# Sorting a step's matmuls by tile shape: quarter taps, masks and scores ahead of the whole taps of the first convolution

## What is computed

```python
stk = _neighborhood(x)                      # 9 shifted views, zero padded
q = einsum('bhwd,de->bhwe', x, Q_P)
k = einsum('bhwkd,de->bhwke', stk, K_P)
v = einsum('bhwkd,de->bhwke', stk, V_P)
scores = einsum('bhwke,bhwe->bhwk', k, q) * mask
alpha = softmax(scores, axis=-1)
t = x + einsum('bhwk,bhwke->bhwe', alpha, v)
t_in = t
t = relu(conv(t, ff1_kernel) + ff1_bias)
t = relu(conv(t, ff2_kernel) + ff2_bias)
t = relu(conv(t, ff3_kernel) + ff3_bias)
return t_in + t
```

## Time and profile before

| | |
|---|---|
| Median of 3 runs | 2202.69 us (2202.68 to 2203.93) |
| The profiled execution | 2203.28 us |
| Its span, first to last instruction | 2201.5 us |
| TensorE busy (PE) | 2143.1 us, 97% of the span |
| VectorE busy | 1875.5 us, 85% |
| ScalarE busy | 1121.7 us, 51% |
| A middle step, first r_product to the next | 32.93 us |
| Granted TensorE clock, mean | 0.997 |

### The profile page before, as it was taken

The page is one execution under the profiler, slowest core; times in us unless marked ns, Lnnn a source line. Parts: engine busy times, 40 slices in busy tenths (PEclk is TensorE's granted clock), DMA queues, the critical chain, the costliest instruction groups (busy, mean ns, idle before and its releaser), DMA issues.

```text
span 2201.5 us, 62613 instructions
## 1 busy us (share of the span) xinstructions
PE 2143.1 (97%) x24057; PEld 1206.6 (55%) x24057; DVE 1875.5 (85%) x2772; ACT 1121.7 (51%) x3059; POOL 17.8 (1%) x28
## 2 busy tenths in 40 slices
PE   3999999999999999999999999999999999999998
PEld 2655555555555555555556555555556555555554
DVE  4888888888888888888878888888888888888886
ACT  2554554554544555555545555545545554554552
POOL 3000000000000000000000000000000000000000
PEclk9999999999999999999999999999999999999999
DMA  5445445445444445455444454454455454454453
GB/s 135 120 145 162 145 138 162 145 137 163 146 138 152 140 153 153 140 151 155 141 145 146 130 174 143 130 173 143 131 172 148 134 165 147 132 165 149 138 158 127
DMA packets 288996, 323.26 MB, mean 147 GB/s; under 512 B 88996, under 2 KB 222948, under 8 KB 282340
## 3 DMA queue, kind: packets, MB, share of 16 engines
q1 hardware_dynamic: 288940, 322.45, 49.0%
HBM read 152.50 MB, written 33.82 MB: 85 GB/s over the span
## 4 chain that ended last, share of the span: by engine, by line
PE 92%; DVE 5%; issue 1%; DMA 1%; SPq 1%; ACT 0%; DVEq 0%; ACTq 0%
PE conv_banks L505 32%; PE conv_banks L530 27%; PE conv_banks L460 16%; PE mix_bank L438 6%; PE score_banks L411 4%; DVE work L893 3%; PE score_banks L423 3%; PE mix_bank L450 3%; PE score_banks L403 1%; DMA work<-w 1%; PE mix_bank L387 0%; ACT relued L720 0%; DVE dt L821 0%; SPq L270 0%; ACT prob L663 0%
## 5 line engine op out<-in xcount | busy, mean ns | idle before, releaser
L505 PE MATMUL conv_banks<-dodd,w3f 128*64 128x512 f32 (+2 forms) x1616 | 499.9, 591 | 4.8 <-DVE work L860 3.1
L505 PE MATMUL conv_banks<-deven,w3f 128*64 128x512 f32 (+2 forms) x1616 | 492.1, 580 | 0.0
L663 ACT ACTIVATE prob<-score_banks,negmax 128x100 f32<-128x100 f32 x1040 | 344.2, 343 | 196.2 <-DVE negmax L783 196.2
L460 PE MATMUL conv_banks<-dt,w1f 128*64 128x256 f32 (+2 forms) x4128 | 384.8, 387 | 8.1 <-DVE work L893 1.4
L530 PE MATMUL conv_banks<-duh,w2h 64*128 64x512 f32 (+1 forms) x1576 | 323.2, 403 | 0.8 <-DVE work L884 0.6
L530 PE MATMUL conv_banks<-duh,w2l 64*128 64x512 f32 (+1 forms) x1576 | 314.5, 392 | 0.0
L460 PEld LDWEIGHTS conv_banks<-dt,w1f 128*64 128x64 f32 (+1 forms) x4128 | 205.1, 135 | 185.8 <-issue 57.9
L530 PE MATMUL conv_banks<-dul,w2h 64*128 64x512 f32 (+1 forms) x1576 | 280.5, 402 | 0.0
L505 PEld LDWEIGHTS conv_banks<-dodd,w3f 128*64 128x64 f32 x1616 | 137.4, 136 | 231.1 <-issue 211.6
L680 ACT COPY probt<-score_banks 100x1024 f32<-100x1024 f32 x130 | 132.0, 1015 | 242.2 <-PE score_banks L423 242.2
L675 ACT COPY rq<-mix_bank 128x512 f32<-128x512 f32 x65 | 38.2, 588 | 406.9 <-PE mix_bank L387 406.8
(11 more groups left out here) (96 smaller groups left out, 2919.1 us busy)
## 6 DMA issues: line engine op xcount, KB each, us to landing
xk<-x_keys SPq DMA_DIRECT2D x66, 800.0 KB
xc<-x_bands SPq DMA_DIRECT2D x66, 650.0 KB, 4.9
xr<-x_bands SPq DMA_DIRECT2D x264, 128.0 KB, 3.4
dodd<-dodd SPq DMA_DIRECT2D x65, 512.0 KB, 5.1
out<-work SPq DMA_DIRECT2D x64, 512.0 KB, 2.7
xs<-x_bands SPq DMA_DIRECT2D x132, 128.0 KB, 3.1
dt<-dt SPq DMA_DIRECT2D x65, 256.0 KB, 2.3
deven<-deven SPq DMA_DIRECT2D x65, 256.0 KB, 5.5
```

The source lines that it names most:

```text
L460: mm = nc.tensor.matmul(bank[(LOWER, UPPER)[o], n * 256 + lo * 64:n * 256 + hi * 64], w1f[i][rows, m, s, o * C:o * C + C], dt[rows, lo + s ...
L505: mm = nc.tensor.matmul(bank[rows, lo_ * 128:hi_ * 128], w3f[:, m, s, odd * C:odd * C + C], source[:, lo_ + s // 2:hi_ + s // 2, m], start ...
L663: last = nc.scalar.activation(prob[:, g % 2, a], score_banks[:, g % 2, a * KEYS:(a + 1) * KEYS], ACT.Exp, bias=negmax[:, g % 2, a:a + 1], ...
```

## The change

- **TensorE, a step with k from 1 to 15.** After r_product and the first masks come the inner quarter taps, the scores of half 0, the second masks, the scores of half 1 and the outer quarter taps, all 64*64. Then all whole taps, inner and outer, and directly behind them the four tiles of the third convolution, all 128*64. The turn of half 0 stands behind the third convolution. Both halves of mix stand together behind the first half of the second convolution. v_product stands behind go_on2 of stream 2 instead of ahead of it.
- **TensorE, steps with k = 0 and DRAIN.** Whole taps stay ahead of quarter taps; both halves of the scores stand between the inner and the outer product. The rest is as above.
- **PSUM.** proj_bank and mix_bank become far_banks, and score_banks near_banks: half 0 has its scores in near_banks, half 1 in far_banks; r_product and v_product write far_banks, mix writes near_banks. negmax, expsum, expinv and prob hold four groups instead of two.
- **Waits.** A semaphore phase_begun, which nothing waits for, is incremented in TensorE's list behind some waits; the wait then stands on that instruction. The dummy matmuls of hold, ahead of the first step, go.
- **ScalarE.** keep_r of half 1 comes ahead of relu_conv2(EVEN); exps of groups 0 to 2 come ahead of relu_conv1 and group 3 behind it; keep_turned of both halves stand together, and keep_y of both halves.
- **VectorE.** max_scores of group 0 comes one place earlier; groups 1 to 3 follow middle1; scale of groups 0 and 1 moves behind the first convolution's inputs. Ahead of the first step all max_scores and scale come before the work on weights.

```diff
             def step(G, k, b, att):
                 if att:
                     r_product(b)
-                    masks()
-                conv1(G, k, b, False, att)
-                if att:
+                    masks(0)
+                await_conv1(G, b, False)
+                if k in (0, DRAIN):
+                    wholes(k, False, True)
+                    quarters(k, False, False)
...
+                else:
+                    pe.sem_inc(phase_begun)
+                    quarters(k, False, True)
+                    pe.wait_ge(r_ready, b * 2 + 1)
+                    pe.sem_inc(phase_begun)
                     scores(b, 0)
-                conv1(G, k, b, True)
-                conv3_tile(G, k, 0)
-                conv3_tile(G, k, 1, (lambda: await_prob(b, 0)) if att else None)
+                    pe.wait_ge(r_ready, b * 2 + 2)
+                    pe.sem_inc(phase_begun)
+                    masks(1)
+                    scores(b, 1)
+                    await_conv1(G, b, True)
+                    pe.sem_inc(phase_begun)
+                    quarters(k, True, True)
+                    wholes(k, False, False)
+                    wholes(k, True, False)
+                for j in range(4):
+                    conv3_tile(G, k, j, (lambda: await_prob(b, 0)) if att and j == 3 else None)
                 if att:
                     turn(b, 0)
-                conv3_tile(G, k, 2, (lambda: await_r(b, 1)) if att else None)
-                if att:
-                    masks()
-                    scores(b, 1)
-                conv3_tile(G, k, 3)
-                if att:
-                    mix(b, 0)
                 begin2(G, k, 0)
                 go_on2(G, k, 0)
                 begin2(G, k, 1, (lambda: await_prob(b, 1)) if att else None)
...
                 end2(G, k, 1)
                 if att:
+                    mix(b, 0)
                     mix(b, 1)
-                begin2(G, k, 2, (lambda: await_y(b)) if att else None)
-                if att:
+                begin2(G, k, 2)
+                go_on2(G, k, 2)
+                if att:
+                    await_y(b)
+                    pe.sem_inc(phase_begun)
                     v_product(b)
-                go_on2(G, k, 2)
                 begin2(G, k, 3)
```

ScalarE's step:

```diff
                 if att:
                     keep_r(b, 0)
                 if p is not None:
                     relu_conv2(G, None, ODD, 1)
+                if att:
+                    keep_r(b, 1)
+                if p is not None:
                     relu_conv2(G, None, EVEN, 1)
-                if att:
-                    keep_r(b, 1)
                 keep_u2(G, k)
```

VectorE ahead of the first step:

```diff
-            max_scores(0, 0)
-            max_scores(0, 1)
-            scale(0, 0)
-            scale(0, 1)
+            for g in range(GROUPS):
+                max_scores(0, g)
+            for g in range(GROUPS):
+                scale(0, g)
             dve.wait_ge(w_in, 80)
...
-            max_scores(0, 2)
-            max_scores(0, 3)
-            scale(0, 2)
-            scale(0, 3)
```

More of the change, by code:

```diff
@@ L372, in _ @@
         def _(pe):
-            def hold(bank):
-                nc.tensor.matmul(bank[:, 0:2], eye16_sb[:], window_sb[:, 0:2], start=True, stop=True)
             def await_band(b):
@@ L402, in masks @@
                         to = (UPPER if rows is LOWER else LOWER) if swap else rows
-                        nc.tensor.matmul(banks[n][to], eye16_sb[rows, rows], mask[rows], start=True, stop=False)
+                        nc.tensor.matmul(banks[half][n][to], eye16_sb[rows, rows], mask[rows], start=True, stop=False)
             def scores(b, half):
@@ L410, in scores @@
                             to = (UPPER if rows is LOWER else LOWER) if swap else rows
-                            mm = nc.tensor.matmul(banks[n][to, a], rq[rows, patch],
+                            mm = nc.tensor.matmul(banks[half][n][to, a], rq[rows, patch],
                                                   xc[rows, :, patch * PATCH:patch * PATCH + HALO],
@@ L422, in turn @@
                     for n, rows in enumerate((LOWER, UPPER)):
-                        last = nc.tensor.transpose(score_banks[0:KEYS, n, a * C:(a + 1) * C],
-                                                   prob[rows, a // GROUP, a % GROUP], eye_sb[rows, rows])
+                        last = nc.tensor.transpose(score_banks[half][0:KEYS, n, a * C:(a + 1) * C],
+                                                   prob[rows, 2 * half + a // GROUP, a % GROUP], eye_sb[rows, rows])
                         if a == HALF - 1:
@@ L464, in tap1, with await_conv1 @@
                     mm.then_inc(conv1_done, 1)
-            def conv1(G, k, b, outer, att=False):
+            def await_conv1(G, b, outer):
                 pe.wait_ge(dt_done, b * 2 - (0 if outer else 1))
@@ L579, in _ @@
             pe.wait_ge(xs_in, 32)
-            hold(proj_bank)
             r_product(0)
-            await_r(0, 0)
-            hold(score_banks[:, 0])
-            masks()
+            masks(0)
+            pe.wait_ge(r_ready, 1)
             scores(0, 0)
-            await_prob(0, 0)
-            hold(score_banks[:, 0])
-            turn(0, 0)
-            await_r(0, 1)
-            hold(score_banks[:, 0])
-            masks()
-            scores(0, 1)
-            mix(0, 0)
-            await_prob(0, 1)
-            hold(score_banks[:, 0])
-            turn(0, 1)
-            mix(0, 1)
+            pe.wait_ge(r_ready, 2)
+            masks(1)
+            scores(0, 1)
+            for half in range(2):
+                await_prob(0, half)
+                turn(0, half)
+            for half in range(2):
+                mix(0, half)
             await_y(0)
-            hold(proj_bank)
             v_product(0)
@@ L733, in _ @@
                 keep_r(0, half)
-            exps(0, 0)
-            exps(0, 1)
-            keep_turned(0, 0)
-            exps(0, 2)
-            exps(0, 3)
-            keep_y(0, 0)
-            keep_turned(0, 1)
-            keep_y(0, 1)
+            for g in range(GROUPS):
+                exps(0, g)
+            for half in range(2):
+                keep_turned(0, half)
+            for half in range(2):
+                keep_y(0, half)
             act.wait_ge(pool_zeroed, 1)
@@ L938, in step @@
                     inputs(G, None, ODD, 0, 1)
-                    inputs(G, None, EVEN, 0, 1)
                 if att:
                     max_scores(b, 0)
+                if p is not None:
+                    inputs(G, None, EVEN, 0, 1)
                 middle1(G, k)
                 if att:
-                    max_scores(b, 1)
+                    for g in range(1, GROUPS):
+                        max_scores(b, g)
                 outer1(G, k)
-                if att:
-                    scale(b, 0)
                 if p is not None:
                     inputs(G, None, EVEN, 1, 1)
-                if att:
-                    scale(b, 1)
-                if p is not None:
                     inputs(G, None, ODD, 1, 1)
```

113 lines of the change are left out of this document (54 added, 59 removed).

## The result

The kernel after takes **2237.48 us** (median; 2235.36 to 2238.97), before 2203.31 beside it: a ratio of 1.0153, 95% interval 1.0138 to 1.0168. It is slower, as forecast; the time is inside the range and 10 us above the predicted 2227. The profiled execution's span is 2236.2 us, 34.7 more than before.

A forecast was written before the change was run, and what follows sets the result against it. TensorE sets the time, with VectorE following at 0.24 us of room. From 2203.28: 56 x 0.50 = +28.0, +3, -2.4, -4.1 gives 2227.8; the median is 0.6 lower, 2227. Range 2209 to 2251.

The forecast's parts named there:

- The forecast's chain: Middle step: keep_r copy, second masks, scores, quarter taps, inner whole taps, keep_u2, then middle1 at 1017.42 instead of 1016.03.
- VectorE's run: Middle step, VectorE from middle1 to scale(b, 3): 14.94 us without gaps, so the last probabilities come at 1032.36.
- restart: TensorE after the last probabilities: resumes 0.06 later, at 1032.42, 0.48 earlier than in before; 0.05 given back on the first pair.
- mix(b, 0) behind the wait: TensorE, second convolution: this mix now follows the last probabilities' wait, adding 0.93 us; the whole step changes by +0.50.
- The decision point: Start of middle1: each 0.1 us before 1017.42 takes 0.1 off the step; at 1016.92 the step is unchanged.
- rival 1: All steps: the whole saving from fewer tile-shape switches arrives, 78.5 us, giving 2124; 12%, mostly part of it, 2124 to 2198.
- the wait for prob: Sign expected in the new profile: TensorE waits for prob ahead of the second turn, about half a us each step.
- k = 1: The four k = 1 steps, 32.34 us in before: the new cycle of 33.4 holds there too; +3 taken for the four.
- k = 0: The four k = 0 steps: inner taps stay first, TensorE still bounds, four switches go; -0.6 each, -2.4.
- The first step: Prologue: VectorE's max and scale for the first band's second half move into a wait for weights; -4.1, bounded by 0 and -5.5.
- two waits as all but met: TensorE in before: first whole tap just after outer(ODD); second-convolution pair needing the last probabilities, 0.24 after scale(b, 3) ends.
- The rule weighed there: TensorE tile-shape changes: the skill says each drains it; 0.15 us a switch, eight fewer, 1.2 us less per middle step.

## Why the prediction was right, and where its sizes were off

**Direction and mechanism: right.** The forecast's chain is in the trace link for link. In the prediction's times: copy ended 1012.79 as said; second masks 1012.93 (said 1012.88); middle1 1017.50 (1017.42); VectorE's run 1045.28 - 1030.34 = 14.94, said 14.94; last probabilities 1032.44 (1032.36); restart 0.06 later, as said; mix(b, 0) behind the wait +0.93 (2.01 instead of 1.08 from mix to the next group), as said. The decision point holds too: with middle1 0.23 earlier the step was 0.26 shorter, and with middle1 at 6.50 behind the R product (1015.9 in the prediction's times, ahead of 1016.92) part of rival 1's saving came about, with two switches less saved. VectorE's idle 1.4 ahead of middle1 was 1.50, the wait for prob about half a us 0.49 by starts.

**The step was sized 0.13 too small:** +0.63 instead of +0.50. (a) The chain up to middle1 is 0.08 longer, mostly because the masks restart 0.14 behind the copy, not 0.09; the first whole taps start 0.35 behind the last quarter taps where 0.21 is usual, a switch of 0.14, not 0.10; and ScalarE's copy starts some 0.15 behind the inner taps, not 0.10. Shorter rows take the rest back. (b) The pair that carries the wait gives back 0.10 (0.34 to the turn, 0.24 in before), not 0.05. (c) Every second step is 0.1 longer (about 33.5 and 33.6 in turn): VectorE's middle1 starts 0.03 behind the copy's end in the step shown, 0.13 behind it in the next, and so in turn through the loops. The copy and middle1 of the next step:

```profile
1063.23 0.59 ACT L691 COPY m_sb<-conv_banks 128x512 f32<-128x512 f32 x1 [2.56 <-PE conv_banks L451]
```

```profile
1063.95 0.69 DVE L861 TENSOR_TENSOR work<-conv_banks,m_sb 128x512 f32<-128x512 f32 x1 [1.57 <-ACT m_sb L691]
```

I had one value for a restart. (d) v_product behind go_on2 gives 0.05 back. In sum -0.40 at the restart (said -0.48), +0.10, +0.93, -0.05 = +0.58 for the step shown (measured 33.51 - 32.93), and 0.05 more on the mean for (c). 56 x 0.13 = 7 of the 10 us.

**The other terms.** k = 1: +5.0 for the four (said +3). The first and the last of them, at a granted clock of 1.00, go from 32.38 and 32.34 to 33.86 and 33.63, so the new cycle holds there in full. k = 0: -3.7 (said -2.4). Here the prediction read one step of four: the two middle ones of before also hold 3.72 and 3.55 us in which TensorE idles ahead of the next R product without a releaser in the profile, and in after 2.71 and 2.96. Without this idle time three of the four steps are 0.68 or 0.69 shorter, near the 0.6 that was said (the first, at a clock of 0.91 against 1.00, only 0.09); 1.6 of the 3.7 is the idle time, which was not forecast. The first step starts 3.76 earlier (said 4.1): the block is 4.05, the weights landed 0.9 later in this execution, and 0.6 comes back because VectorE no longer waits for the V product there (0.40 in before) and TensorE has no dummy matmuls ahead of the step (0.10). The last, DRAIN step was not in the sum: 1.8 longer, by TensorE's clock (last section). The sum: 56 x 0.63 + 5.0 - 3.7 - 3.8 + 1.8 = 34.6, against 34.7 in the span.

**What the prediction's first part missed.** It named two waits as all but met in before. There is a third, the first tile of the third convolution on middle1 (1017.44 against 1017.31), and the prediction did not show its row. It bore on no term, since middle1 was forecast later anyway, but it means that before was bound by VectorE's chain there too: the two switches taken out ahead of that tile brought nothing, and 0.48 us of VectorE ahead of middle1 cost 0.38. Whether the wait for the last probabilities, with its 0.24 of room, bound before as well was not tested.

**The rule weighed there.** That a change of tiling mode drains TensorE (the Trainium skill, "TensorEngine Tiling (Array Packing)", Key Properties) agrees with the rows between the tap shapes, at 0.10 to 0.14; around the turns there is 0.09 for the two together. By it alone the step would be 1.2 shorter; it became 0.63 longer. The prediction's 15 and 7 switches count a turn as 64*128 and a mix as 128*64; by the profile's names, 64*100 and 100*64, there are 18 and 10, so eight go either way. The other page I read too shortly: the Trainium skill, "Perfetto Trace Analysis", Identifying the Most-Contended Engine, says to begin with the engine of highest occupancy, but also that for TensorE the matmul share is no good measure of how near it is to its limit, and names its share of the peak rate and the share of its weight loads instead. By the weight loads (55% against 85%; VectorE's 85% stands in the same row) it points to VectorE, and the doubled reduction in before, 0.48 of VectorE for 0.38 a step, agrees at the one place that it tests.

## What to carry to other kernels

Before saving work on the busiest engine, list every place where it starts just behind what it needs (0.06 to 0.24 us here), and price a reordering by what moves past those places, not by the engine's sum. When instructions are sorted by kind, see that the ones that another engine's long run waits for stay early: putting one such group back, at the price of two switches, was worth 55 us here. Price a met wait by the distance between starts, not by the idle entry beside it.

## What the hardware showed beside it

TensorE's granted clock fell to 0.50, the lower of its two levels (1.2 GHz), twice near the end of after: for 3 us at the start of DRAIN's third convolution, and for 7 us from the end of DRAIN's second convolution into the short last product (windows, clock third from the end):

```profile
2202.05:2205.05 3.00, 1.04 (x18) 0.85 (x16) 2.90 (x6) 1.30 (x3) 0.00 (x0) 0.96 0.64 172
2205.05:2208.05 3.00, 3.00 (x8) 1.00 (x10) 2.94 (x6) 0.94 (x2) 0.00 (x0) 0.50 0.67 225
...
2221.90:2228.70 6.80, 5.13 (x32) 3.96 (x32) 2.86 (x8) 1.59 (x4) 0.00 (x0) 0.50 0.24 92
```

At the first place in before it was 1.00:

```profile
2169.17:2172.17 3.00, 1.04 (x18) 0.85 (x16) 2.90 (x6) 1.30 (x3) 0.00 (x0) 1.00 0.65 172
2172.17:2175.17 3.00, 3.00 (x14) 1.06 (x16) 2.76 (x4) 0.15 (x1) 0.00 (x0) 1.00 0.74 253
```

TensorE had the same work and nearly the same two waits (1.41, and 1.86 or 1.87 us) just ahead of it in both. In these 3 us it got 8 matmul records done instead of 14. Before has one fall in its last step, of 3.4 us from 2190.95, in the short last product. The kernel with the first reduction doubled has TensorE's code of after there; its profile shows 1.00 through both stretches, and its time from the last R product to the end is 3.5 us shorter (66.6 against 70.1), 1.5 of it over the first fall and 2.0 from the second on. So the falls come and go between executions of the same code; what decides it is not settled here.
